# A decoder layer on one core: scores issued ahead of the PV in front of them, late row work placed anew, and a tail on ScalarE

## The chip, the cores and the metric

The kernel runs on one core of one Trainium2 chip. The metric is the device time of one execution in microseconds (us). The core has five engines with a queue each: PE (TensorE, matrix products), DVE (VectorE), ACT (ScalarE), POOL (GpSimd) and SP (SyncE, which only issues DMAs). They run in parallel and wait for each other through semaphores.

## The reference

The input `x` is 8 batches x 256 rows x 512 features, float32; `ctx` has the same shape.

```python
x = layernorm(x + attention(x))        # 16 heads of 32, softmax over 256 keys, then Wo
r_t = decay * r_{t-1} + ctx_t**2       # per feature, a recurrence along the 256 rows
x = layernorm(x + x * r)
g, u = x @ gate_w.T, x @ up_w.T        # 2048 wide; the three weights are cubic splines
x = layernorm(x + (silu(g) * u) @ down_w.T)
```

## The kernel before, in words

Matrix products keep float32 accuracy by splitting each operand into a high and a low part; each product is three matmuls (lines 303 to 305). The order of the work on every engine is written out by hand, as one function for each piece and engine (`pe_...`, `act_...`, `dve_...`, `pool_...`); each engine takes its queue strictly in that order.

**Attention.** The loop runs over batches `b` = 0 to 7. A batch has four quarters `m` = 0 to 3 of four heads each. A quarter is a chain over the engines:

- S on PE (`pe_s`, line 478): the scores of four heads into four banks of PSUM; minus the maximum of each row on DVE (`dve_max`, line 821); the exponential with row sums on ACT (`act_exp`, line 665);
- T on PE (`pe_t`, line 490): 16 transposes of the probabilities; copies back by ACT (line 677, head group 0) and DVE (line 835, three of them, `dve_heads`);
- R on PE (`pe_r`, line 498): the inverse row sums, spread by DVE (`dve_inverse`, lines 827 and 830), transposed; PV on PE (`pe_pv`, line 512); the product with the inverse on DVE (`dve_y`, line 785), then its high part on ACT (`act_yh`, line 673).

Between these steps PE has other work to cover the chain: the Q, K and V products of the next batch, Wo of the last one, and single matmuls for the spline weights (`pe_extra`). In batch 7 there is no next batch (`proj` is false). The recurrence is one scan per 128 features on DVE (`dve_scan`, line 896), four for a batch. POOL does the rest of the layer norms of a batch: `pool_norm1`, `pool_times`, `pool_scaled` and `pool_norm2`. DVE supplies them: `dve_stats(b, 0)` and `(b, 1)` give the mean and variance that norm1 and norm2 wait for, `dve_size(b)` the scale. SP stores the rows that norm2 finishes to DRAM (`x`, line 1070).

**FFN.** Four blocks `n` of 512 rows, two batches each; a block has eight steps `g` of 256 of the 2048 features, written (n, g). A step makes gate and up (`pe_gate_up`), silu on ACT, the product with up on DVE (`dve_hm`, line 1398), its high part on ACT and low part on DVE (line 1402), and the down product (`pe_down`), which runs one step behind. In block 0 a step also holds up to four *jobs*: each builds a piece of weights from spline coefficients. A job of the down weights needs a table, `makers_out`, that POOL fetches (`pool_makers_out(g)`, lines 1150 and 1151). `AHEAD_JOBS` of them are done before the first step. SP loads the rows of a block again (`x_in`, line 1228), to be transposed by PE (line 1165). POOL loads the block's residual rows, 1 MB, by `pool_res(n)` (line 1490); DVE adds the result of down to them (`dve_add`, line 1408), in the first step of the block that follows. Two of the four adds stand ahead of the second `dve_hm` of that step.

**Tail.** For the last block: add, statistics and `dve_out` (line 1426) per 128 rows on DVE, root and inverse on POOL (lines 1638 and 1640), and four stores that POOL issues at the end (line 1482).

## Time and profile before

| | us |
|---|---|
| median of 3 runs | 684.94 (684.87 to 685.00) |
| the profiled execution | 685.51 |
| its span | 683.7 |
| PE busy | 656.8 (96%) |
| DVE busy | 449.5 (66%) |
| ACT busy | 347.7 (51%) |
| POOL busy | 294.3 (43%) |
| mean granted clock of PE | 0.995 |

The span is the time from the first to the last instruction in the trace; 1.8 us of the execution lie outside it. Busy time is summed per engine. The end of a matmul in the trace is modelled: two that follow one another overlap in it (a 512-column matmul lasts 0.39 us in a row, and the next starts 0.23 us after it). So distances are read from start to start. The projections run to 63.6 us together with batch 0, batches 1 to 6 to 326.5, batch 7 to 367.3, first FFN pieces to 385.5, block 0 of the FFN to 458.5, and blocks 1 to 3 to 673.4, PE's last matmul.

### The profile page before, as it was taken

What the parts mean: (1) busy time and instruction counts of PE and PEld (TensorE: products, weight loads), DVE (VectorE), ACT (ScalarE), POOL (GpSimd) and SP (SyncE); (2) the same over time, 40 slices, a digit from 0 to 9 for tenths busy, and PEclk for the clock granted to TensorE, in tenths of its full rate; (3) what the DMA queues carried; (4) which work ended last, traced back from release to release, by engine and by line L of the source; (5) the groups of instructions that cost most, each with busy time, mean ns of one, the idle gap of its engine ahead of it and who ended that gap; (6) DMA issues with size and microseconds to landing.
All of it is one profiled execution on the core that took longest, in us unless ns stands there. A gap on an engine that the chain in (4) does not pass through costs nothing.

```text
span 683.7 us, 12025 instructions
## 1 busy us (share of the span) xinstructions
PE 656.8 (96%) x4312; PEld 533.8 (78%) x4312; DVE 449.5 (66%) x826; ACT 347.7 (51%) x1002; POOL 294.3 (43%) x351
## 2 busy tenths in 40 slices
PE   9999999999999999999988799999999999999993
PEld 9597887878888788788865577888888888888883
DVE  3567687698686877878778688666544555354434
ACT  5566546637466565656667556552334233333230
POOL 1764486886638767594674836100100001000103
PEclk9999999999999999999999999999999999999997
DMA  9621020030220311121112672741193317340301
GB/s 329 221 80 62 1 87 7 2 125 1 94 62 2 133 52 32 63 72 41 40 65 47 159 173 72 210 105 40 35 239 78 81 32 198 72 101 0 124 1 61
DMA packets 22010, 58.06 MB, mean 85 GB/s; under 512 B 4032, under 2 KB 7232, under 8 KB 21056
## 3 DMA queue, kind: packets, MB, share of 16 engines
q1 hardware_dynamic: 16720, 44.45, 22.5%
q0 software_dynamic: 4944, 12.32, 5.9%
q8 instruction: 35, 0.57, 0.3%
q10 hardware_dynamic: 288, 0.52, 0.2%
q14 instruction: 23, 0.19, 0.1%
HBM read 32.11 MB, written 8.39 MB: 59 GB/s over the span
## 4 chain that ended last, share of the span: by engine, by line
PE 78%; DVE 12%; ACT 6%; issue 2%; POOL 1%; DVEq 0%; POOLq 0%; ACTq 0%
PE bank L303 19%; PE bank L305 18%; PE bank L304 18%; PE bank L490 6%; ACT probs L665 5%; PE bank L478 4%; DVE recurrence_T L896 4%; PE bank L512 4%; DVE minus_max L821 3%; PE bank L1191 2%; PE bank L1096 2%; DVE probsT L835 2%; PE bank L529 1%; PE bank L316 1%; PE bank L498 1%
## 5 line engine op out<-in xcount | busy, mean ns | idle before, releaser
L665 ACT ACTIVATE probs<-bank,minus_max 128x256 f32<-128x256 f32 x256 | 117.3, 486 | 23.8 <-DVE minus_max L821 23.8
L303 PE MATMUL bank<-down,hidden_hi_lo 128*128 128x512 f32 x256 | 100.7, 393 | 1.5 <-DVE hidden_hi_lo L1402 1.5
L305 PE MATMUL bank<-down,hidden_hi_lo 128*128 128x512 f32 x256 | 100.5, 392 | 0.0
L304 PE MATMUL bank<-down,hidden_hi_lo 128*128 128x512 f32 x256 | 100.0, 391 | 0.0
L821 DVE TENSOR_REDUCE minus_max<-bank 128x2 f32<-128x512 f32 x128 | 79.3, 681 | 16.3 <-PE bank L478 16.3
L1398 DVE TENSOR_TENSOR hidden<-bank,silu 128x512 f32<-128x512 f32 x64 | 44.1, 689 | 60.9 <-PE bank L305 58.9
L1356 ACT ACTIVATE silu<-bank 128x512 f32<-128x512 f32 x64 | 38.3, 598 | 82.2 <-PE bank L305 81.3
L1402 DVE TENSOR_TENSOR hidden_hi_lo<-hidden,hidden_hi_lo 128x512 fp32r<-128x512 f32 x64 | 45.5, 711 | 40.9 <-ACT hidden_hi_lo L1369 40.8
L490 PE MATMUL bank<-ident,probs 128*128 128x128 f32 x512 | 65.5, 275 | 6.2 <-ACT probs L665 5.9
L1476 POOL TENSOR_TENSOR ffn_var_eps<-ffn_mean_var,constants 128x4 f32<-128x4 f32 x3 | 0.6, 196 | 156.5 <-DVE ffn_mean_var L1418 156.5
L490 PEld LDWEIGHTS bank<-ident,probs 128*128 128x128 f32 x512 | 56.6, 141 | 14.2 <-ACT probs L665 12.0
L1369 ACT CAST hidden_hi_lo<-hidden 128x512 fp32r<-128x512 f32 x64 | 39.8, 622 | 52.3 <-DVE hidden L1398 52.3
L835 DVE COPY probsT<-bank 128x512 f32<-128x512 f32 x96 | 60.1, 680 | 4.8 <-PE bank L490 4.7
L303 PEld LDWEIGHTS bank<-down,hidden_hi_lo 128*128 128x128 f32 x256 | 48.1, 188 | 11.5 <-DVE hidden_hi_lo L1402 1.9
L305 PEld LDWEIGHTS bank<-down,hidden_hi_lo 128*128 128x128 f32 x256 | 48.0, 188 | 10.3
L665 ACT ACTIVATION_READ_ACCUMULATOR probs<-bank,minus_max 128x1 f32 x256 | 55.9, 219 | 0.0
L304 PEld LDWEIGHTS bank<-down,hidden_hi_lo 128*128 128x128 f32 x256 | 48.1, 188 | 9.7
L303 PE MATMUL bank<-xT_hi_lo,wq_hi 128*128 128x256 f32 x128 | 38.7, 303 | 1.1 <-DVE spline_coef_T_down L773 0.4
L303 PE MATMUL bank<-xT_hi_lo,wk_hi 128*128 128x256 f32 x128 | 38.9, 304 | 0.0
L512 PE MATMUL bank<-probsT,V 128*32 128x256 f32 x512 | 36.8, 385 | 0.4 <-ACT inverse_by_query L680 0.4
L478 PE MATMUL bank<-k_heads,q_heads 32*128 32x256 f32 x512 | 36.7, 400 | 0.0
L305 PE MATMUL bank<-xT_hi_lo,wq_lo 128*128 128x256 f32 x128 | 36.1, 282 | 0.0
(170 smaller groups left out, 1610.8 us busy)
## 6 DMA issues: line engine op xcount, KB each, us to landing
features_by_group<-features_by_cell SPq DMA_DIRECT2D x128, 128.0 KB, 2.4
ctx_squared_T<-in_ctxT SPq DMA_DIRECT2D x8, 512.0 KB, 3.3
xres<-in_x SPq DMA_DIRECT2D x8, 512.0 KB, 4.6
x_in<-x SPq DMA_DIRECT2D x16, 256.0 KB, 3.1
x_residual<-x POOLq DMA_DIRECT2D x4, 1024.0 KB, 8.1
out_x<-x_residual POOLq DMA_DIRECT2D x16, 256.0 KB, 2.8
xin_T<-in_xT SPq DMA_DIRECT2D x7, 512.0 KB, 3.9
x<-x_rows SPq DMA_DIRECT2D x7, 512.0 KB, 4.1
```

What stands on the lines that cost most here:

```text
L303: nc.tensor.matmul(out, wh, xh, start=first, stop=False)
L304: nc.tensor.matmul(out, wh, xl, start=False, stop=False)
L305: return nc.tensor.matmul(out, wl, xh, start=False, stop=last)
L478: last = nc.tensor.matmul(S[g][:, t * T:(t + 1) * T], qk[0][at, m, t * P:(t + 1) * P], qk[1][at, m, :], start=True, stop=True)
L490: last = nc.tensor.transpose(S[g][:, kt * T + t * P:kt * T + (t + 1) * P], probs[:, g, t, kt * P:(kt + 1) * P], ident[:])
L512: last = nc.tensor.matmul(MI[g * DH:(g + 1) * DH, 0:T], V[:, kt, h * DH:(h + 1) * DH], probsT[:, g, kt, :], start=kt == 0, stop=kt == TT - 1)
L665: inc(nc.scalar.activation(probs[:, g, t, :], S[g][:, t * T:(t + 1) * T], ACT.Exp, bias=nmax[:, g, t:t + 1], accum_out=rsum[:, t, g:g + 1] ...
L821: inc(nc.vector.tensor_reduce(nmax[:, g, :], S[g][:].rearrange("p (t k) -> p t k", t=TT), AX.X, ALU.max, negate=True), "max")
L835: inc(nc.vector.tensor_copy(probsT[:, g, :, :], S[g][:].rearrange("p (k t) -> p k t", k=2)), "ptv")
L1369: inc(nc.scalar.copy(hid[:, g % 2, 0, j, :], hm[:]), "hh")
L1398: inc(nc.vector.tensor_tensor(hm[:], U[:], sg[:], ALU.mult), "hm")
L1402: inc(nc.vector.tensor_tensor(hid[:, g % 2, 1, j, :], hm[:], hid[:, g % 2, 0, j, :].bitcast(F32), ALU.subtract), "hl")
```

## The change

1. *S before PV.* On PE, S of quarter m+1 is issued ahead of PV of quarter m. DVE takes the maxima of quarter m+1 ahead of `dve_y` of m, and ACT makes the high part of y inside the exponentials of the next quarter, ahead of the fourth head.
2. *Scan.* The four scans of batches 0 to 6 go from behind `dve_heads(2)` to ahead of `dve_inverse(2)`; those of batch 7 go behind job 16, after the batch.
3. *Row work of batches 6 and 7.* The table of places:

| | before | now |
|---|---|---|
| `dve_stats(6, 1)` | ahead of the FFN | end of step (0, 1) |
| `dve_size(6)` | batch 7 | behind job 17 |
| `dve_stats(7, 0)` | end of (0, 0) | end of (0, 2) |
| `dve_size(7)` | end of (0, 2) | end of (0, 5) |
| `dve_stats(7, 1)` | end of (0, 3) | end of (0, 7) |
| `pe_rs(7)`, `act_rs1(7)` | ahead of features 2 and 3 | behind job 18 |

4. *Makers.* POOL's transfers `pool_makers_out(2)` to `(7)` stand at other places between the norms, and `pool_res(0)`, which was last, still is, but now directly behind `pool_norm2(7)`.
5. *Wo.* The last low part of Wo (`wo_lo`) is made inside the maxima of quarter 1 of batch 0.
6. *Jobs.* 20 instead of 19 are done ahead; step (0, 0) has its job elsewhere.
7. *Tail.* The last normalization is an ACT instruction (identity with scale and bias) per 128 rows, for which POOL makes minus mean times inverse as a third small operation; SP issues the four stores, each when its rows are there.

```diff
+
+        pe_s(pe, b, 1)
         if b == 0:
             pe_fold_o(pe, 3)
         pe_pv(pe, b, 0)
-
-        pe_s(pe, b, 1)
         pe_q(pe, b, 2)
         pe_k(pe, b, 2)
         pe_q(pe, b, 3)
...
             act.wait_ge(s["max"], 16 * b + 4 * m + g + 1)
             for t in range(TT):
                 inc(nc.scalar.activation(probs[:, g, t, :], S[g][:, t * T:(t + 1) * T], ACT.Exp,
@@ -708,7 +710,6 @@
         if post:
             act_rs1(act, b - 1)
         act_extra(act, b, 0)
-        act_yh(act, b, 0)
 
...
         if b == 0:
-            for m in range(MT):
+            for m in range(MT - 1):
                 dve_weight_lo(dve, "o", m)
+        dve_max(dve, b, 1)
         dve_y(dve, b, 0)
-        dve_max(dve, b, 1)
         dve_extra(dve, b, 0)
         if post:
             dve_stats(dve, b - 1, 0)
         dve_inverse(dve, b, 1)
         dve_heads(dve, b, 1)
 
+        dve_max(dve, b, 2)
         dve_y(dve, b, 1)
-        dve_max(dve, b, 2)
         dve_extra(dve, b, 1)
-        if not proj:
-            dve_scan(dve, b, range(2))
+        if proj:
+            dve_scan(dve, b)
         dve_inverse(dve, b, 2)
         dve_heads(dve, b, 2)
-        if proj:
-            dve_scan(dve, b, range(KT))
-        else:
+
+        dve_max(dve, b, 3)
+        dve_y(dve, b, 2)
+        if not proj:
             dve_x2l(dve, 0, 0, B_)
             dve_x2l(dve, 0, 1, C_)
-
-        dve_y(dve, b, 2)
-        dve_max(dve, b, 3)
         dve_extra(dve, b, 2)
-        if post:
+        if post and proj:
             dve_size(dve, b - 1)
-        if not proj:
-            dve_scan(dve, b, range(2, KT))
         dve_inverse(dve, b, 3)
         dve_heads(dve, b, 3)
...
+    def dve_scan(dve, b):
+        dve.wait_ge(s["csq"], 2 * b + 2)
+
+        wait(dve, "rs", 2 * b)
+        for k in range(KT):
             inc(nc.vector.tensor_tensor_scan(rsT[:, k, :], dec[:, k:k + 1].to_broadcast([P, T]),
...
-        if post:
+        if post and b < B - 1:
             pool_scaled(pool, b - 1)
...
-    AHEAD_JOBS = 2 * NG + 3
+    AHEAD_JOBS = 2 * NG + 4
...
             if n == 0:
-                pe.wait_ge(s["wld"], 2 * JT * g + 1)
+                wait(pe, "wld", 2 * JT * g)
+                pe.wait_ge(s["wl"], AHEAD_JOBS)
...
-        i = AHEAD_JOBS + (2 * JT * g - 2 + k if g else k)
-        return i if n == 0 and i < NJOB and (g or k < 2) else None
+        i = AHEAD_JOBS + (2 * JT * g - 3 + k if g else k)
+        return i if n == 0 and i < NJOB and (g or k < 1) else None
...
@@ -1337,13 +1334,13 @@
         pe_gate_up(pe, n, g, 0)
         pe_turn(pe, n, g, 0)
         pe_down(pe, prev, 0)
-        pe_fill(pe, n, g, 0)
+        if prev:
+            pe_fill(pe, n, g, 0)
         pe_down(pe, prev, 1)
-        if prev:
-            pe_fill(pe, n, g, 1)
+        pe_fill(pe, n, g, 1)
         pe_turn(pe, n, g, 1)
         pe_gate_up(pe, n, g, 1)
-        pe_fill(pe, n, g, 2 if prev else 1)
+        pe_fill(pe, n, g, 2 if prev else 0)
...
-        act_fill_hi(act, n, g, 0)
         if before(n, g):
+            act_fill(act, n, g, 0)
+            act_fill_hi(act, n, g, 0)
             act_fill(act, n, g, 1)
             act_turn(act, n, g, 1)
             act_fill_hi(act, n, g, 1)
             act_silu(act, n, g, 1)
+            act_fill(act, n, g, 2)
+            act_hh(act, n, g, 1)
         else:
             act_silu(act, n, g, 1)
-            act_fill(act, n, g, 1)
-            act_fill_hi(act, n, g, 1)
-        act_fill(act, n, g, 2)
-        act_hh(act, n, g, 1)
+            act_hh(act, n, g, 1)
+            act_fill(act, n, g, 0)
+            act_fill_hi(act, n, g, 0)
...
     def dve_out(dve, n, t):
-        if n < NB - 1:
-            dve.wait_ge(s["rstd"], n + 1)
-        else:
-            wait(dve, "rstd", NB + t)
+        dve.wait_ge(s["rstd"], n + 1)
...
-        dve_fill(dve, n, g, 0)
-        if ends:
-            dve_add(dve, n - 1, 1)
-        dve_fill_lo(dve, n, g, 0)
         if before(n, g):
+            dve_fill(dve, n, g, 0)
+            if ends:
+                dve_add(dve, n - 1, 1)
+            dve_fill_lo(dve, n, g, 0)
             dve_fill(dve, n, g, 1)
             dve_turn(dve, n, g, 1)
             dve_fill_lo(dve, n, g, 1)
             dve_hm(dve, n, g, 1)
+            dve_fill(dve, n, g, 2)
+            dve_hl(dve, n, g, 1)
         else:
             dve_hm(dve, n, g, 1)
-            dve_fill(dve, n, g, 1)
-            dve_fill_lo(dve, n, g, 1)
-        dve_fill(dve, n, g, 2)
-        dve_hl(dve, n, g, 1)
+            dve_hl(dve, n, g, 1)
+            dve_fill(dve, n, g, 0)
+            dve_fill_lo(dve, n, g, 0)
...
         if n == 0:
-            if g == 0:
+            if g == 1:
+                dve_stats(dve, B - 2, 1)
+            elif g == 2:
                 dve_stats(dve, B - 1, 0)
-            elif g == 2:
+            elif g == 5:
                 dve_size(dve, B - 1)
-            elif g == 3:
+            elif g == 7:
                 dve_stats(dve, B - 1, 1)
...
+            pe_rs(pe, B - 1, 0)
+            pe_rs(pe, B - 1, 1)
+            pe.wait_ge(s["ws"], 2 * NG + 3)
+            pe_job(pe, 2 * NG + 3, X)
...
-            act_fh(act, 0, 0, B_)
-            act_fh(act, 0, 1, C_)
-            act_rs1(act, B - 1)
-            act_fh(act, 0, 2, A_)
-            act_fh(act, 0, 3, B_)
+            for q, out in enumerate((B_, C_, A_, B_)):
+                act_fh(act, 0, q, out)
             act_job_hi(act, 2 * NG - 1)
             for i in range(2 * NG, AHEAD_JOBS):
                 act_job(act, i, X)
                 act_job_hi(act, i)
+                if i == AHEAD_JOBS - 2:
+                    act_rs1(act, B - 1)
...
+            for t in range(BT):
+                act.wait_ge(s["nm"], t + 1)
+                inc(nc.scalar.activation(res[:, t, :], res[:, t, :], ACT.Identity, bias=fnm[:, t:t + 1], scale=frstd[:, t:t + 1]), "yout")
...
-            dve_fl(dve, 0, 3, B_)
+            for q, out in enumerate((B_, C_, A_, B_)):
+                dve_fl(dve, 0, q, out)
             dve_job(dve, 2 * NG, X)
+            dve_scan(dve, B - 1)
             dve_r1(dve, B - 1, 0)
             dve_job(dve, 2 * NG + 1, X)
+            dve_size(dve, B - 2)
             dve_r1(dve, B - 1, 1)
             dve_job(dve, 2 * NG + 2, X)
+            dve_job(dve, 2 * NG + 3, X)
...
                     dve_step(dve, n, g)
@@ -1592,9 +1594,6 @@
                 dve_out_stats(dve, NB - 1, t)
                 dve.wait_ge(s["bn"], BT * (NB - 1) + t + 1)
                 inc(nc.vector.bn_aggr(fmv[:, t, :], fst6[:, t, :]), "mv")
-                if t:
-                    dve_out(dve, NB - 1, t - 1)
-            dve_out(dve, NB - 1, BT - 1)
...
             for i in range(2 * NG - 1, AHEAD_JOBS):
                 pool_job_lo(pool, i)
+            pool_scaled(pool, B - 2)
+            pool_makers_out(pool, 2)
             pool_norm2(pool, B - 2)
-            pool_makers_out(pool, 2)
+            pool_makers_out(pool, 3)
             pool_norm1(pool, B - 1)
+            pool_makers_out(pool, 4)
             pool_times(pool, B - 1)
-            pool_makers_out(pool, 3)
-            pool_makers_out(pool, 4)
+            pool_makers_out(pool, 5)
+            pool_makers_out(pool, 6)
             pool_scaled(pool, B - 1)
-            pool_makers_out(pool, 5)
+            pool_makers_out(pool, 7)
             pool_norm2(pool, B - 1)
-            pool_makers_out(pool, 6)
-            pool_makers_out(pool, 7)
             pool_res(pool, 0)
...
@@ -1638,9 +1638,9 @@
                 inc(nc.gpsimd.tensor_tensor(fve[:, t:t + 1], fmv[:, t, 1:2], half[:, 0, 0:1], ALU.add), "ve")
                 pool.wait_ge(s["ve"], NB + t)
                 inc(nc.gpsimd.tensor_tensor(frstd[:, t:t + 1], fve[:, t:t + 1], half[:, 2, 0:1], ALU.pow), "rstd")
-            for t in range(BT):
-                pool_out(pool, NB - 1, t)
-            pool.wait_ge(s["out"], 16 * BT * NB)
+                pool.wait_ge(s["rstd"], NB + t)
+                inc(nc.gpsimd.tensor_scalar(fnm[:, t:t + 1], fmv[:, t, 0:1], frstd[:, t:t + 1], -1.0, ALU.mult, ALU.mult), "nm")
+            pool.wait_ge(s["out"], 16 * BT * (NB - 1))
...
+            for t in range(BT):
+                sp.wait_ge(s["yout"], BT * (NB - 1) + t + 1)
+                inc(sp.dma_start(out_v[:, BT * (NB - 1) + t, :], res[:, t, :]), "last", 16)
+            sp.wait_ge(s["last"], 16 * BT)
```

**PE, batch 1, around the scores of quarter 1.** L478 are the scores, L512 is PV, L529 and L402 are pieces of other work. Before:

```order
L498 MATMUL bank<-ident,row_sum_inverse_wide 128x128 x2
L529 MATMUL bank<-ident,recurrence_T 128x128 x4
L402 MATMUL bank<-ident,spline_coef_rows 128x128 x4
L512 MATMUL bank<-probsT,V 32x256 x8
L478 MATMUL bank<-k_heads,q_heads 128x256 x8
L303 MATMUL bank<-xT_hi_lo,wq_hi 128x256
```

Now:

```order
L498 MATMUL bank<-ident,row_sum_inverse_wide 128x128 x2
L529 MATMUL bank<-ident,recurrence_T 128x128 x4
L402 MATMUL bank<-ident,spline_coef_rows 128x128 x4
L478 MATMUL bank<-k_heads,q_heads 128x256 x8
L512 MATMUL bank<-probsT,V 32x256 x8
L303 MATMUL bank<-xT_hi_lo,wq_hi 128x256
```

The two groups have changed places; nothing else moved there.

**DVE, batch 1, quarters 2 and 3.** Before (L896 in the profile is the scan):

```order
L827 RECIPROCAL row_sum_inverse<-row_sum 128x8
L830 COPY row_sum_inverse_wide<-row_sum_inverse 128x256
L835 COPY probsT<-bank 128x512 x3
L896 SCALAR_TENSOR_TENSOR recurrence_T<-decay,ctx_squared_T 128x256 x4
L785 TENSOR_TENSOR heads_out<-bank,inverse_by_query 128x256
L821 TENSOR_REDUCE minus_max<-bank 128x2 x4
```

Now (the scan is L892, the inverse L828 and L831, the copies L836):

```order
L822 TENSOR_REDUCE minus_max<-bank 128x2 x4
L784 TENSOR_TENSOR heads_out<-bank,inverse_by_query 128x256
L772 CAST spline_coef_T_up<-bank 128x512
L892 SCALAR_TENSOR_TENSOR recurrence_T<-decay,ctx_squared_T 128x256 x4
L828 RECIPROCAL row_sum_inverse<-row_sum 128x8
L831 COPY row_sum_inverse_wide<-row_sum_inverse 128x256
L836 COPY probsT<-bank 128x512 x3
L822 TENSOR_REDUCE minus_max<-bank 128x2 x4
L784 TENSOR_TENSOR heads_out<-bank,inverse_by_query 128x256
```

The scans stand ahead of the inverse and the three copies of quarter 2 now, behind the maxima of that quarter.

**POOL, from the first norm of batch 7 to the residual load.** Before (of the small operations of `pool_norm2(7)` the last is shown):

```order
L957 TENSOR_SCALAR residual_odd<-residual_odd,mean_var,rstd 128x512 x2
L965 TENSOR_TENSOR residual_odd<-residual_odd,recurrence_plus_one 128x512 x2
L1150 DMA makers_out<-in_makers 128x256
...
L995 TENSOR_TENSOR rstd_kept<-rstd,keep 128x2
L1002 TENSOR_SCALAR recurrence_plus_one<-residual_odd,mean_var,rstd_kept 128x512 x2
L1150 DMA makers_out<-in_makers 128x256
L1151 DMA masks_out<-in_masks 128x256
L1150 DMA makers_out<-in_makers 128x256
L1151 DMA masks_out<-in_masks 128x256
L1490 DMA x_residual<-x 128x2048
```

Now:

```order
L998 TENSOR_SCALAR x_rows<-residual_even,mean_var,rstd_kept 128x512 x2
L1146 DMA makers_out<-in_makers 128x256
L1147 DMA masks_out<-in_masks 128x256
L947 TENSOR_TENSOR var_eps<-mean_var,constants 128x2
L949 TENSOR_TENSOR rstd<-var_eps,constants 128x2
L953 TENSOR_SCALAR residual_odd<-residual_odd,mean_var,rstd 128x512 x2
...
L991 TENSOR_TENSOR rstd_kept<-rstd,keep 128x2
L998 TENSOR_SCALAR recurrence_plus_one<-residual_odd,mean_var,rstd_kept 128x512 x2
L1488 DMA x_residual<-x 128x2048
```

The second norm of batch 6 (`x_rows`) is now followed directly by table 3, which stood behind `pool_times(7)`. Tables 6 and 7 went ahead of the second norm of batch 7, which now stands directly ahead of the residual load.

## Rows read from the trace of the kernel before

The columns of a timeline are the start in us, the duration in us, engine, line, operation, output<-input, and in brackets the idle time ahead of it with what ended it. The columns of a windows view are the stretch, its length, then busy time (and instructions) of PE, PE's weight load, DVE, ACT and POOL, the granted clock of PE, the DMA share and GB/s.

**Rows 1.** windows of PE's span; length, busy of each engine, clock, DMA share, GB/s
```profile
63.60:326.50 262.90, 258.77 (x2189) 212.05 (x2188) 201.62 (x378) 157.16 (x554) 182.67 (x197) 1.00 0.15 50
326.50:385.50 59.00, 51.19 (x375) 37.90 (x373) 46.34 (x94) 38.92 (x121) 36.24 (x48) 1.00 0.25 66
385.50:458.50 73.00, 71.93 (x340) 58.17 (x341) 55.61 (x111) 43.88 (x97) 27.11 (x34) 1.00 0.53 142
458.50:673.40 214.90, 214.88 (x953) 175.48 (x951) 107.09 (x180) 71.89 (x120) 13.51 (x25) 1.00 0.32 82
```

**Rows 2.** waits of PE, 20 to 326.5 us: total, times, longest
```profile
PE bank L490 <- ACT probs L665: 2.8, 11, 0.3
...
PE bank L303 <- DVE spline_coef_T_down L773: 0.4, 2, 0.2
```

**Rows 3.** timeline of PE in batch 1: start, duration, operation
```profile
91.62 1.91 PE L490 MATMUL bank<-ident,probs 128*128 128x128 f32 x16
...
94.08 0.39 PE L498 MATMUL bank<-ident,row_sum_inverse_wide 128*128 128x128 f32 x2
...
95.78 1.07 PE L512 MATMUL bank<-probsT,V 128*32 128x256 f32 x16
...
102.25 0.66 PE L490 MATMUL bank<-ident,probs 128*128 128x128 f32 x4
103.16 0.66 PE L490 MATMUL bank<-ident,probs 128*128 128x128 f32 x4 [0.25 <-ACT probs L665]
```

**Rows 4.** timeline of DVE in batch 1
```profile
94.50 5.73 DVE L896 TENSOR_TENSOR_SCAN recurrence_T<-decay,ctx_squared_T 128x256 f32<-128x256 f32 x4
```

**Rows 5.** the scan's line L896: min/median/max ns over the program
```profile
L896 DVE TENSOR_TENSOR_SCAN recurrence_T<-decay,ctx_squared_T x32: 657/1026/2505, 51.5 to 363.0; 128x256 f32<-128x256 f32 x32
```

**Rows 6.** timeline of DVE in FFN step (0, 1)
```profile
396.52 0.68 DVE L1211 TENSOR_TENSOR features_by_cell<-bank,features_by_cell 128x512 fp32r<-128x512 f32 x1
```

**Rows 7.** timeline of POOL, second norm of batch 7
```profile
419.62 0.19 POOL L983 TENSOR_TENSOR var_eps<-mean_var,eps 128x2 f32<-128x2 f32 x1 [2.69 <-DVE mean_var L801]
...
426.96 0.61 POOL L1150 DMA_DIRECT2D makers_out<-in_makers  x1
...
437.77 0.53 POOL L1490 DMA_DIRECT2D x_residual<-x  x1
```

**Rows 8.** DMA issues, 386 to 391 us: KB each, us to landing
```profile
x_in<-x SPq DMA_DIRECT2D x2, 256.0 KB, 4.3
```

**Rows 9.** timeline of PE at the end of step (0, 2)
```profile
404.81 0.60 PE L1165 MATMUL bank<-ident,x_in 128*128 128x128 f32 x4
```

**Rows 10.** timeline of DVE at the end of block 0
```profile
457.97 0.69 DVE L1211 TENSOR_TENSOR features_by_cell<-bank,features_by_cell 128x512 fp32r<-128x512 f32 x1
...
462.10 1.44 DVE L1408 TENSOR_TENSOR x_residual<-bank,x_residual 128x512 f32<-128x512 f32 x2
464.24 0.69 DVE L1398 TENSOR_TENSOR hidden<-bank,silu 128x512 f32<-128x512 f32 x1 [0.69 <-PE bank L305]
```

**Rows 11.** timeline of PE, group 1 of block 1
```profile
467.47 0.39 PE L303 MATMUL bank<-features_by_group,spline_coef_T_up 128*128 128x512 f32 x1
```

**Rows 12.** DMA issues, 436 to 447 us
```profile
x_residual<-x POOLq DMA_DIRECT2D x1, 1024.0 KB, 8.5
```

**Rows 13.** DMA issues, 640 to 652 us
```profile
x_residual<-x POOLq DMA_DIRECT2D x1, 1024.0 KB, 5.0
```

**Rows 14.** windows at the start and after the last matmul
```profile
1.50:7.70 6.20, 6.20 (x29) 6.20 (x30) 1.66 (x3) 3.44 (x5) 0.07 (x3) 1.00 0.91 299
...
673.40:676.70 3.30, 0.00 (x0) 0.00 (x0) 3.16 (x8) 0.00 (x0) 1.32 (x4) 1.00 0.00 0
676.70:683.70 7.00, 0.00 (x0) 0.00 (x0) 0.80 (x2) 0.00 (x0) 3.14 (x6) 0.50 0.40 150
```

**Rows 15.** timelines of the end: DVE
```profile
676.44 0.52 DVE L1426 TENSOR_SCALAR x_residual<-x_residual,ffn_mean_var,ffn_rstd 128x512 f32<-128x512 f32 x1
```

**Rows 16.** timelines of the end: POOL
```profile
677.58 2.34 POOL L1482 DMA_DIRECT2D out_x<-x_residual  x4
```

26 lines of the change are left out of this document (8 added, 18 removed).

## The prediction

> **What bounds the kernel now.** First the windows of the trace, for PE's busy time in each stage. Blocks 1 to 3 of the FFN have no hole: 214.88 us busy of 214.9. Block 0 loses 1.1 of 73.0, batches 1 to 6 lose 4.1 of 262.9, and only batch 7 with the first FFN pieces loses much, 7.8 of 59.0 [rows 1]. So PE bounds nearly everything, no matmul is added or removed, and the change can win little ahead of the tail. It can lose without limit wherever it puts a wait in front of PE. Second, the waits of PE, for what ends them: in the batches the transposes, held up by ACT's exponentials, and the products behind a spline coefficient that DVE casts [rows 2]. Third, the timelines where the change moves something, above all the last DVE and POOL work of block 0. Fourth, the end after the last matmul, 10.3 us in which PE does nothing.
>
> All sums are against the profiled execution, 685.51 us (span 683.7 and 1.8 around it). It lies 0.57 above the median 684.94; I take that off at the end.
>
> **S before PV, batches 0 to 6.** A held group of four transposes starts 0.91 us after the one before it; 16 transposes without a wait last 1.91 us, 0.109 from start to start and 0.44 a group [rows 3]. So each of the 11 waits before 326.5 costs 0.47: 5.2 us. PV lasts 1.07 us, 1.0 to the start of the next [rows 3]; with S ahead of it the exponentials start that much earlier, and in batch 1 three waits of 0.47, 1.4 in all, were there to gain. The six spline waits of 0.2 idle cost 0.35 each, start to start: 2.1 more, since the cast no longer stands behind a late y. Gain at most 7.3. (The windows show 4.1 idle there, because the modelled ends of matmuls cover part of each hole; starts are the better measure.)
>
> Against it, the scan. In batch 1 four scans take 5.73 us behind the copies of quarter 2, and PE meanwhile does other products [rows 4]. Moved ahead of the inverse, they start at about 89.4 (behind maxima and the cast, y no longer in the way) and end at 95.1 at that pace; then 0.7 for the reciprocal and the spread row. R is issued at 94.08 [rows 3], so PE waits 1.8, and S of quarter 3, which needs the copies, 0.2 more. At the shortest scan, 0.66, they end at 92.0 and nothing waits; the median is 1.03 [rows 5]. Per batch 0 to 2.0. I take 1.1 in batches 1, 2 and 3, 0.3 in batch 0 and nothing in 4 to 6, where the same reading leaves slack: 3.6 in all; 0 to 9 as bounds. Net -3.7; with 0.3 for the last low part of Wo, which comes earlier into reach of batch 0, I take **-4.0** (-7 to +2).
>
> The scan has two inputs in the SBUF memory. The trace shows it between 0.66 and 2.51 us for one size [rows 5], the long ones beside POOL operations. The Trainium skill, "SBUF — State Buffer", "Who interferes with whom", says that a DVE instruction with two SBUF inputs contends with a GpSimd instruction that reads SBUF, one blocking the other. The trace agrees. By that rule the price of the moved scan depends on what POOL does at the new place, and the upper bound of each batch stands; by a fixed cost per scan it would be nothing.
>
> **Batch 7 to the end of step (0, 1).** The scans leave the batch, which frees waits of some 1.5, but they now stand with `dve_size(6)` (1.2 and two small ones) between jobs 16 and 19 on DVE, and job 19 itself is new ahead of the first down product: 2.7 + 1.6 of DVE work in front of a PE that has only Wo and two jobs left. I set the one against the other: +0.1 (-3 to +3; all that is idle there is 7.8 [rows 1]). In steps (0, 0) and (0, 1): job 20 placed late +0.2, POOL's norm of batch 7 no longer beside DVE -0.6, `dve_stats(6, 1)` at the end of (0, 1) +1.0. Sum **+0.7**.
>
> **Table 3 and x_in, step (0, 2).** `dve_stats(6, 1)` now runs behind the last feature copy of (0, 1), which starts at 396.52 [rows 6]: two statistics and aggregates, 1.65 us, so its result is there at about 398.2. `pool_norm2(6)` waits for it and takes what it takes for batch 7: 419.62 to 426.96, 7.3 [rows 7]. Behind it, from 405.5, stand table 3 on POOL and on SP the store of batch 6 with two `x_in` loads behind it, which land after 4.3 [rows 8]. PE wants `x_in` at 404.81 [rows 9] and table 3 just ahead of it; they come at about 409 to 410. With the 0.7 of above already late, PE waits **+3.5** (2 to 4.5).
>
> **Steps (0, 2) to (0, 7).** Statistics of batch 7 at the end of (0, 2): +0.3. Table 4 is issued behind norm1(7), which waits for those statistics; it lands some 1.5 after job 32 wants it: +1.5 (0 to 2.5). `dve_size(7)` and table 7: +0.7 together (0 to 1). Sum **+2.5**.
>
> **The residual of block 0.** This is the largest term. Before, `pool_norm2(7)` was done at 426.96 and the load was issued at 437.77 [rows 7], 24 us before DVE wanted it, at 462.10 [rows 10]. Now `dve_stats(7, 1)` comes at the end of step (0, 7), after the copy that ends at 458.66 [rows 10], and adds 1.65: 460.3. Norm2 takes 7.3, to 467.7. Only then does POOL issue the load. It lands 8.5 after its issue [rows 12] with the store of batch 7 and two `x_in` beside it, and the same two are released with it now: 476.2. DVE is strictly in order: two adds (1.44), then `dve_hm` of step (1, 0), which releases the bank that "up" of group 1 fills. It ended at 464.93 and will end at 478.3. PE wants the bank at 467.47 [rows 11]: 10.9 lost. The down product then waits for the low part, 0.7 more than "up" of 0.7 hides. Together 11.6, against a nominal time that already moved with the terms above; nothing else shortens it, as DVE follows PE's banks by under 1 us there (its wait of 0.69 in [rows 10]). Bounds: the last of the four residual loads, alone in the queues, landed in 5.0 [rows 13], which makes 8.1; 1 us more than 8.5 makes 12.6. I take **+11.7**.
>
> **The clock.** PE's granted clock was 1.00 (2.4 GHz) through the 3.3 us after the last matmul and 0.50 (1.2 GHz) in the 7.0 behind them [rows 14]. An idle PE of some 11 us would meet this. At the start, 29 matmuls of the size of a transpose took 6.2 us [rows 14], 0.21 each against 0.109 in [rows 3]. If the same comes back, half of 6.2 us is lost, 3.1. But the one group "up" falls into the wait, and the shorter waits of batch 7, 7.8 us in all, cost no clock [rows 1]. **+2.0** (0 to 3.1). The Trainium skill, "TensorE: Matmul & The Clock Gate", "Part 1: The HAM clock gate", says that the default state is throttled and activity releases it. By that rule the loss comes for certain after the long wait, and the sum would be 1.1 higher.
>
> **Tail.** Three of DVE's outputs stand between adds and statistics, 0.52 us each; the third starts at 676.44 [rows 15], right behind the last aggregate. The two ahead of that, 0.43 each from start to start, delay it: -0.9. POOL then takes 0.4 and 0.5, and a third small one of 0.3 to 0.5 comes in: +0.4. ACT's normalization replaces DVE's (0.55); ACT's casts of 128x512 took 0.6: 0. POOL issued four stores in a row, 2.34 us, from 677.58 [rows 16], and the last landed 3.1 after its own issue. SP issues each when its rows are there, so three of the issues (1.6) lie beside other work. The end comes after the landing either way. -2.1, and -0.3 as POOL's own wait is off the path: **-2.4** (-1.5 to -3). An activation table might have to be loaded; the trace has none on ACT between silu and identity-like copies in the FFN, so I take nothing for it.
>
> **Sum.** -4.0 + 0.7 + 3.5 + 2.5 + 11.7 + 2.0 - 2.4 = +14.0; 685.5 + 14.0 = 699.5 profiled, less 0.57: **698.9 us**, slower by 2.0%.
>
> **Rivals.**
> A, *faster*: the residual load is no wait. For that DVE would have to finish step (0, 7) 11 us or more ahead of PE's need, or POOL to reach the norm earlier. From 11.6 us of slack on it costs nothing; below, the difference. Then the table and `x_in` of step (0, 2) would be covered as well, and the time is 684.9 - 4.0 + 0.7 + 0.5 - 2.4 = 679.7. Against it: DVE follows PE by under 1 us in [rows 10]. Chance 0.06.
> B, *the load is short and the clock holds*: 8.1 in place of 11.7, and no clock term: 684.9 + 14.0 - 3.6 - 2.0 = 693.3. For it: the load that is alone lands in 5.0 [rows 13]. Against it: the same companions as at 437.77. Chance 0.24.
> C, *the scans eat the batches*: the moved scan costs 2.0 in each of batches 1 to 5, 10.0 in place of 3.6: 684.9 + 14.0 + 6.4 = 705.3. For it: POOL is as busy there in batches 4 and 5. Chance 0.12.
> D, *the clock falls at both long waits*, also at the 3.5 of step (0, 2), which is as long as the 3.3 that passed at full clock: 3.1 twice in place of 2.0: 703.1. Chance 0.08.
> The forecast, with its neighbours of 2 us either side: 0.49. The rest, 0.01, near no change.
>
> The change may also not do all that it says in the batches: if S still waits for what PV waited for, the gain of 5.2 is gone; that gives 704.1 and counts with C.
>
> **How the numbers follow.** Low end: B with a further 3 from the bounds of the batches, 690. High end: C with 0.7 more, 706. The forecast's own range is 695.5 to 702.5. A measurement tells 0.2% (1.4 us) from no change here. Faster only by A and by an edge of the batches' gain: 0.07; within 0.2%: 0.02; slower: 0.91.
>
> **What would show it.** Right: a DVE `x_residual` add in the first step of block 1 that waits some 10 us for the DMA, with the residual load issued at about 467 plus the shift, directly behind norm2; PE idle for that long ahead of "up" of group 1; a granted clock under 1 behind it; another PE wait of about 3 us at `x_in` or job 28; the waits of transposes on ACT gone from the batches, and new ones at line 498 on the inverse row in batches 1 to 3; a tail shorter than 8.3 us from the last matmul. Wrong: the load lands before the add is due. Then the sum falls by two thirds and more, and everything hangs on batches and tail, which favour the change.

## The result, and the profile after

The changed kernel takes 701.19 us (median of 4 runs, 697.83 to 702.46), against 684.97 for the kernel before in the same comparison: ratio 1.0229, 95% interval 1.0194 to 1.0265. It is slower by 16.2 us; the whole interval lies above 1, and whether it is 2% or a little less stays open. The profiled execution took 701.36 with a span of 699.6.

How far the changed kernel is ahead of or behind the one before, read from the start of the same DVE instruction in both traces (maxima in the attention, `dve_hm` in the FFN):

| place | shift, us |
|---|---|
| batch 2, quarter 0 | -2.9 |
| batch 4, quarter 0 | -5.9 |
| batch 6, quarter 2 | -9.9 |
| batch 7, quarter 0 | -7.0 |
| first down product | -6.8 |
| FFN step (0, 2), second half | -7.2 |
| (0, 3), first half | -0.9 |
| (0, 3), second half | +6.9 |
| (0, 7), second half | +8.9 |
| (1, 0), second half | +21.6 |
| (1, 1), second half | +21.0 |
| (3, 7), second half | +19.4 |
| end of the span | +15.8 |

From batch 6 on, 0.5 us of each entry belong to the profiled execution of the kernel before: its PV of batch 5 (282.7 to 283.6) ran 0.5 longer than in e4, e6, e9 and e10, whose work there is the same. Without it the end is at +16.3, as the medians have it.

Attention gains 7 to 10 us, three places in the FFN lose 27, and blocks 1 to 3 and the tail give 5 back. The waits of PE in the changed kernel name the three places (columns as in [rows 2]):

```profile
PE bank L303 <- DVE hidden L1396: 10.2, 1, 10.2
PE bank L1161 <- DMA x_in<-x: 5.9, 1, 5.9
PE bank L1092 <- DMA makers_out<-in_makers: 5.8, 2, 4.6
...
PE bank L498 <- DVE row_sum_inverse_wide L831: 1.9, 1, 1.9
PE bank L478 <- DVE probsT L836: 1.7, 3, 1.2
...
PE bank L490 <- ACT probs L667: 1.1, 3, 0.6
```

The last row answers to the first of [rows 2]: of the transposes' waits on the exponentials almost nothing is left. L1161 is the transpose of `x_in`, L1092 a job with table 3.

**The residual load.** POOL, the changed kernel:

```profile
469.16 0.19 POOL L979 TENSOR_TENSOR var_eps<-mean_var,eps 128x2 f32<-128x2 f32 x1 [15.90 <-DVE mean_var L800]
...
472.17 4.15 POOL L998 TENSOR_SCALAR recurrence_plus_one<-residual_odd,mean_var,rstd_kept 128x512 f32<-128x512 f32 x2
476.27 0.61 POOL L1488 DMA_DIRECT2D x_residual<-x  x1
```

DVE and PE behind it:

```profile
470.37 0.69 DVE L1400 TENSOR_TENSOR hidden_hi_lo<-hidden,hidden_hi_lo 128x512 fp32r<-128x512 f32 x1 [0.69 <-ACT hidden_hi_lo L1366]
484.58 1.29 DVE L1406 TENSOR_TENSOR x_residual<-bank,x_residual 128x512 f32<-128x512 f32 x2 [13.53 <-DMA x_residual<-x]
485.79 0.68 DVE L1396 TENSOR_TENSOR hidden<-bank,silu 128x512 f32<-128x512 f32 x1
```

```profile
486.52 0.80 PE L303 MATMUL bank<-features_by_group,spline_coef_T_up 128*128 128x512 f32 x1 [10.18 <-DVE hidden L1396]
```

The load is issued 5.2 us after the add could have run (471.06, behind the row at 470.37) and lands 8.3 later. DVE stands 13.5 us in front of the add, with the `hm` that PE waits for behind it in its queue. These rows answer to [rows 7, 10, 11].

**Step (0, 2).** POOL and SP's queue in the changed kernel:

```profile
390.55 0.19 POOL L979 TENSOR_TENSOR var_eps<-mean_var,eps 128x2 f32<-128x2 f32 x1 [9.92 <-DVE mean_var L800]
...
397.89 0.62 POOL L1146 DMA_DIRECT2D makers_out<-in_makers  x1
```

```profile
397.97 0.33 SPq L1066 DMA_DIRECT2D x<-x_rows  x1
398.39 1.24 SPq L1224 DMA_DIRECT2D x_in<-x  x2
399.67 10.55 SPq L1216 DMA_DIRECT2D features_by_group<-features_by_cell  x16
410.26 1.08 SPq L1224 DMA_DIRECT2D x_in<-x  x2
```

PE:

```profile
401.99 0.77 PE L1092 MATMUL bank<-spline_coef_T_down,makers_out 128*128 128x256 f32 x2 [4.56 <-DMA makers_out<-in_makers]
...
417.31 1.12 PE L1161 MATMUL bank<-ident,x_in 128*128 128x128 f32 x4 [5.91 <-DMA x_in<-x]
```

POOL waits 9.9 us for the statistics of batch 6 and then needs 7.3 for norm2. Table 3 is issued behind it, at 397.89, and PE waits 4.6 for it. The store and the first `x_in` pair are late as well, and so are the 16 feature transfers behind them; only behind these comes the second pair, which PE wants at 411.4. It lands 7.0 after its issue. In the kernel before the order on SP is the same, but the 16 transfers start at 391.74, the second pair is issued at 405.55, and PE uses it without a wait at 411.98.

**The clock.** Windows of the changed kernel:

```profile
350.50:353.10 2.60, 0.07 (x4) 0.01 (x1) 2.60 (x6) 2.60 (x13) 0.00 (x0) 1.00 0.00 0
353.10:356.50 3.40, 3.38 (x18) 3.22 (x19) 1.39 (x5) 3.37 (x10) 1.50 (x2) 0.61 0.00 0
...
397.30:402.00 4.70, 0.14 (x2) 0.04 (x1) 1.03 (x2) 0.41 (x2) 1.77 (x3) 0.96 0.72 205
402.00:411.30 9.30, 8.96 (x38) 7.22 (x38) 5.30 (x12) 3.75 (x8) 3.64 (x4) 0.84 1.04 215
411.30:417.30 6.00, 0.10 (x1) 0.00 (x0) 0.87 (x2) 0.37 (x1) 5.01 (x5) 0.83 0.98 205
417.30:418.60 1.30, 1.29 (x5) 1.25 (x6) 0.00 (x0) 0.13 (x1) 0.00 (x0) 0.50 0.05 14
418.60:423.00 4.40, 4.40 (x14) 3.52 (x13) 2.76 (x5) 2.65 (x6) 0.40 (x1) 0.60 0.00 0
...
476.00:486.50 10.50, 0.35 (x2) 0.00 (x0) 1.89 (x3) 0.00 (x0) 0.89 (x2) 0.70 0.90 250
486.50:492.00 5.50, 5.47 (x16) 4.17 (x17) 3.18 (x5) 1.74 (x3) 0.00 (x0) 0.65 1.06 217
```

The granted clock fell from 2.4 to 1.2 GHz at each of the three long waits, also at the one of 4.6 us, and came back some us into the work that followed: 0.84 over 9.3 us, 0.50 and 0.60 over 5.7, 0.65 over 5.5. Work in these stretches ran longer by the missing share: 1.5, 2.4 and 1.9 us, 5.8 in all. The Trainium skill, "TensorE: Matmul & The Clock Gate", "Part 1: The HAM clock gate", says that the throttled clock is the default and that activity releases it; the trace agrees at these three places.

The first two rows are batch 7, where the clock fell as well (0.61 over 3.4 us), behind a wait of 2.6 that had another of 1.2 ahead of it. The traces with this wait of 2.6 (the changed kernel, e1, e2 and e8) all show it, but batch 7 can lose clock without the change too. In the profiled execution of the kernel before there is no fall; in e6, which has the same instructions and the same waits there (0.8 and 1.05, against 0.8 and 1.04), the clock is half for 3.4 us. Before, then e6, the windows and the PV in them:

```profile
364.90:368.30 3.40, 3.03 (x22) 1.41 (x22) 2.93 (x7) 1.88 (x6) 3.01 (x5) 1.00 0.00 0
365.33 1.95 PE L512 MATMUL bank<-probsT,V 128*32 128x256 f32 x16 [0.22 <-ACT inverse_by_query L680]
```

```profile
364.90:368.30 3.40, 3.40 (x18) 1.73 (x15) 2.20 (x4) 1.02 (x4) 2.32 (x5) 0.50 0.00 0
364.63 2.81 PE L512 MATMUL bank<-probsT,V 128*32 128x256 f32 x16 [0.22 <-ACT inverse_by_query L680]
```

So between executions of the same work the clock falls behind a wait of 1 us or does not. It costs 0.9 us there, and the executions of the kernel before that were taken beside the experiments stand in two groups that fit: 684.7 to 685.4 with a mean clock of 0.994 to 0.996, and 685.7 to 686.0 with 0.991 to 0.994 (one of 1075 us at 0.556, a slow one, is left out).

**The tail.** SP and ACT at the end of the changed kernel, and the landing of the four stores:

```profile
692.60 4.86 SPq L1694 DMA_DIRECT2D out_x<-x_residual  x4
```

```profile
696.30 0.81 ACT L1563 ACTIVATE x_residual<-x_residual,ffn_minus_mean,ffn_rstd 128x512 f32<-128x512 f32 x1 [0.71 <-POOL ffn_minus_mean L1642]
```

```profile
out_x<-x_residual SPq DMA_DIRECT2D x4, 256.0 KB, 2.0
```

SP issues the four over 4.9 us, each when its rows are there, and they land in 2.0 us (median; 2.8 in the kernel before, from POOL).

### The profile page after: what moved, and what is told of

It is laid out like the page before. It is cut to its first block, busy times and chain, and to the rows that moved or that the text cites. A ratio compares the mean times of both kernels' runs of the same rounds, so it can differ in the third digit from the quotient of the medians.

```text
span 699.6 us, 12030 instructions
## 1 busy us (share of the span) xinstructions
PE 654.8 (94%) x4312; PEld 538.0 (77%) x4312; DVE 441.9 (63%) x821; ACT 349.6 (50%) x1006; POOL 293.0 (42%) x352
## 4 chain that ended last, share of the span: by engine, by line
PE 81%; DVE 7%; POOL 3%; DMA 3%; ACT 2%; issue 2%; SPq 2%; DVEq 0%; POOLq 0%; ACTq 0%
PE bank L303 19%; PE bank L304 18%; PE bank L305 18%; PE bank L490 8%; PE bank L478 5%; PE bank L512 4%; PE bank L1187 2%; SPq L1216 1%; PE bank L1092 1%; DMA x_residual<-x 1%; PE bank L498 1%; DMA x_in<-x 1%; PE bank L1161 1%; PE bank L402 1%; PE bank L529 1%
## 5 line engine op out<-in xcount | busy, mean ns | idle before, releaser
L667 ACT ACTIVATE probs<-bank,minus_max 128x256 f32<-128x256 f32 x256 | 118.7, 487 | 41.0 <-DVE minus_max L822 41.0
L836 DVE COPY probsT<-bank 128x512 f32<-128x512 f32 x96 | 60.3, 681 | 10.3 <-PE bank L490 10.3
L490 PE MATMUL bank<-ident,probs 128*128 128x128 f32 x512 | 63.1, 277 | 1.1 <-ACT probs L667 1.1
L490 PEld LDWEIGHTS bank<-ident,probs 128*128 128x128 f32 x512 | 58.6, 143 | 4.2 <-ACT probs L667 1.8
L303 PEld LDWEIGHTS bank<-down,hidden_hi_lo 128*128 128x128 f32 x256 | 48.9, 191 | 10.7 <-DVE hidden_hi_lo L1400 1.3
L305 PEld LDWEIGHTS bank<-down,hidden_hi_lo 128*128 128x128 f32 x256 | 48.6, 190 | 10.5
L304 PEld LDWEIGHTS bank<-down,hidden_hi_lo 128*128 128x128 f32 x256 | 48.8, 191 | 9.2
L917 POOL TENSOR_TENSOR yT_lo<-heads_out,yT_hi 128x256 fp32r<-128x256 f32 x24 | 20.0, 835 | 60.5 <-ACT yT_hi L675 60.5
L478 PE MATMUL bank<-k_heads,q_heads 32*128 32x256 f32 x512 | 36.7, 399 | 2.3 <-DVE probsT L836 1.7
L682 ACT COPY inverse_by_query<-bank 128x256 f32<-128x256 f32 x32 | 11.9, 373 | 52.0 <-PE bank L498 52.0
```

Of the source, the lines that this page charges most:

```text
L303: nc.tensor.matmul(out, wh, xh, start=first, stop=False)
L304: nc.tensor.matmul(out, wh, xl, start=False, stop=False)
L305: return nc.tensor.matmul(out, wl, xh, start=False, stop=last)
L478: last = nc.tensor.matmul(S[g][:, t * T:(t + 1) * T], qk[0][at, m, t * P:(t + 1) * P], qk[1][at, m, :], start=True, stop=True)
L490: last = nc.tensor.transpose(S[g][:, kt * T + t * P:kt * T + (t + 1) * P], probs[:, g, t, kt * P:(kt + 1) * P], ident[:])
L667: inc(nc.scalar.activation(probs[:, g, t, :], S[g][:, t * T:(t + 1) * T], ACT.Exp, bias=nmax[:, g, t:t + 1], accum_out=rsum[:, t, g:g + 1] ...
```

## The experiments

All ratios are to the kernel before, run beside the same group: e1 to e4 (median 685.03), e5 to e8 (685.25), e9 to e11 (684.97). Differences of times from two groups carry these 0.3 us. The diffs are excerpts; "..." marks what is left out.

**e1: row work of batches 6 and 7, and POOL's order of norms, tables and residual load, as before; all else as changed** (parts 3 and 4 without `pe_rs(7)` and `act_rs1(7)`).

```diff
-        if post and proj:
+        if post:
             dve_size(dve, b - 1)
...
-            if g == 1:
-                dve_stats(dve, B - 2, 1)
+            if g == 0:
+                dve_stats(dve, B - 1, 0)
             elif g == 2:
-                dve_stats(dve, B - 1, 0)
-            elif g == 5:
                 dve_size(dve, B - 1)
-            elif g == 7:
+            elif g == 3:
                 dve_stats(dve, B - 1, 1)
...
+            dve_stats(dve, B - 2, 1)
...
-            dve_size(dve, B - 2)
...
-            pool_scaled(pool, B - 2)
+            pool_norm2(pool, B - 2)
             pool_makers_out(pool, 2)
-            pool_norm2(pool, B - 2)
+            pool_norm1(pool, B - 1)
+            pool_times(pool, B - 1)
             pool_makers_out(pool, 3)
-            pool_norm1(pool, B - 1)
...
```

> The changed kernel with the row work of batches 6 and 7 (statistics, sizes, scaled) and POOL's order of norms, tables and residual load as before; all else as changed. Theory W (three late DMAs behind the late row work cost about 21 us of PE and the clock some 5 more): the waits at table 3, at both pairs of x_in and at the residual add go, 24 of 701.2, so 677 (675 to 680), and PE's granted clock is 1.00 through block 0. Theory J (the twentieth job ahead and the new order of step (0, 0) cost the time): the time stays above 690.

676.90 us, ratio 0.9878 (0.9863 to 0.9893). All three long waits are gone, as theory W has it, and theory J's 690 falls. The new places of the row work and of what POOL does behind it cost 24.3 us; e1 puts both back, so it does not share this out between statistics and tables. W's clock of 1.00 through block 0 was missed by one stretch: it was half from 385.7 to 389.1, behind a wait of 1.9 for a job's weights on DVE.

**e2: only the residual load put ahead.**

```diff
+            pool_res(pool, 0)
             pool_norm2(pool, B - 1)
-            pool_res(pool, 0)
```

> The changed kernel with only the residual load of block 0 ahead of the second norm of batch 7. Theory W: the wait of 10.2 us ahead of up of group 1 goes and the half-speed stretch behind it (1.9), so 689 (687.5 to 690.5), with the waits of step (0, 2) unchanged. Rival L (the load lands late whatever its place, because the queues are full there): 698 to 701.

689.58 us, ratio 1.0055 (1.0037 to 1.0074): 11.6 less than the changed kernel, from two lines exchanged, and inside W's range. L falls. The waits of step (0, 2) remain: 4.5 and 5.0 in its trace.

**e3: the swap alone on the kernel before.**

```diff
+        pe_s(pe, b, 1)
         if b == 0:
             pe_fold_o(pe, 3)
         pe_pv(pe, b, 0)
-
-        pe_s(pe, b, 1)
...
+        dve_max(dve, b, 1)
         dve_y(dve, b, 0)
-        dve_max(dve, b, 1)
```

> The kernel before with part 1 of the change alone (S ahead of PV, maxima ahead of y, high part of y ahead of the fourth head, Wo's last low part): scan, row work, jobs and tail as before. Theory S (the swap itself gains the batches): 5 to 7 of the 9.9 us, so 678 to 680. Rival R (the scan's move gains them, since the scan of quarter 2 holds the maxima of quarter 3): the waits of the last transposes of batches 1 to 3 stay, and the time is 682 to 684.

685.98 us, ratio 1.0012 (1.0002 to 1.0021): nothing gained. Both numbers missed; R's mechanism was seen, though. The waits of the transposes stay (6.7 us, 18 of them; 5.9 and 19 before), since DVE still takes the scan ahead of the maxima of quarter 3:

```profile
95.15 5.56 DVE L897 TENSOR_TENSOR_SCAN recurrence_T<-decay,ctx_squared_T 128x256 f32<-128x256 f32 x4
100.63 2.45 DVE L822 TENSOR_REDUCE minus_max<-bank 128x2 f32<-128x512 f32 x4
```

**e4: the tail alone on the kernel before**, the diff of part 7.

> The kernel before with the tail alone (last normalization on ACT, stores by SP). Theory T (the profile's 3.6 us are the tail's own): 681.4 (681 to 681.8). Rival (some of it came with the shifted PE): 682.5, my forecast's 2.4.

679.25 us, ratio 0.9916 (0.9901 to 0.9931): 5.8 less, where 3.6 was expected. From the last matmul on the trace gains the 3.6. The other 2.2 lie in FFN steps that the edit does not touch: their 512-column matmuls follow each other faster (e6, e9, e10).

**e5: the moved scan alone on the kernel before.**

```diff
-        if not proj:
+        if proj:
+            dve_scan(dve, b, range(KT))
+        else:
             dve_scan(dve, b, range(2))
         dve_inverse(dve, b, 2)
         dve_heads(dve, b, 2)
-        if proj:
-            dve_scan(dve, b, range(KT))
-        else:
+        if not proj:
             dve_x2l(dve, 0, 0, B_)
             dve_x2l(dve, 0, 1, C_)
```

> The kernel before with the scans of batches 0 to 6 ahead of the inverse and the copies of quarter 2, and nothing else. The swap alone gained nothing in the batches (+1.3 in its trace) and both together gained 9.9 up to batch 6. Theory P (each needs the other: with the scan where it was, the maxima of quarter 3 still come late, and with the scan moved but S behind PV the copies come late for PV): 684 to 687. Rival R (the scan alone gains it): 676 to 678.

689.32 us, ratio 1.0056 (1.0039 to 1.0073): slower by 4.1, above P's 684 to 687; R falls. PE waits at line 498 for the row that DVE spreads behind the scan, 8.8 us in five waits: 1.5, 2.3, 2.3 and 1.7 in batches 0 to 3, and 1.0 in batch 7 that was there before. Neither half gains; the two together gain 9.9 up to batch 6. Batch 1 shows how. DVE in e5:

```profile
91.14 5.55 DVE L896 TENSOR_TENSOR_SCAN recurrence_T<-decay,ctx_squared_T 128x256 f32<-128x256 f32 x4
```

DVE in the changed kernel, and POOL beside it:

```profile
87.75 3.29 DVE L892 TENSOR_TENSOR_SCAN recurrence_T<-decay,ctx_squared_T 128x256 f32<-128x256 f32 x4
```

```profile
88.36 1.18 POOL L917 TENSOR_TENSOR yT_lo<-heads_out,yT_hi 128x256 fp32r<-128x256 f32 x1 [1.59 <-ACT yT_hi L675]
89.50 1.00 POOL L905 CAST xT_hi_lo<-xin_T 128x512 fp32r<-128x512 f32 x1
```

With S and the maxima early, the scan starts 3.4 us earlier than in e5. There POOL is idle at first, and the four scans take 3.3 instead of 5.6. In batches 1 to 6 the four take 3.3 to 3.4 in the changed kernel; in e5 they take 5.6 in batches 1 to 3 and 2.4 in 4 to 6, where no wait at line 498 arises. The Trainium skill, "SBUF — State Buffer", "Who interferes with whom", says that a DVE instruction with two SBUF inputs contends with a GpSimd instruction that reads SBUF, and that the order of issue decides which one is held up. The trace fits: in the changed kernel POOL's operations beside the scans are the long ones (1.18 and 1.00, where the same two take 0.74 and 0.61 in e5, ahead of its scans), and the scans are not. Which of the two has to wait was not tested by itself.

**e6: 16 unused bytes.**

```diff
-    fve, frstd = sb("ffn_var_eps", [P, BT]), sb("ffn_rstd", [P, BT])
+    fve, frstd, unused = (sb(n, [P, BT]) for n in ("ffn_var_eps", "ffn_rstd", "unused"))
```

> The kernel before with one more small tile of 16 bytes for each partition, allocated where the changed tail has ffn_minus_mean, and used by nothing. In the tail-alone kernel the 512-column matmuls of the FFN followed each other in 0.227 us in place of 0.229, all through blocks 1 to 3. Theory A (the tile shifts the addresses of all the large tiles behind it, and PE reads them faster there): 0.227 here too and 2.2 to 2.7 us less, 682.5. Rival C (it comes from the code or the semaphores of the tail): 684.9.

682.75 us, ratio 0.9964 (0.9951 to 0.9977): 2.2 to 2.5 us from a tile that nothing uses. A holds.

**e7: swap, moved scan and tail on the kernel before** (e3, e5 and e4 together).

> The kernel before with swap, moved scan of batches 0 to 6 and tail; row work, makers, jobs ahead and the residual load as before. If the gains of the batches (9.9 until batch 6, of which 2 to 3 go again in batch 6) and of the tail-alone kernel (5.8) add: 671 (669 to 673). If batch 7 and the first steps need the new places of the change too: 674 to 677, like the kernel with only the row work put back.

673.79 us, ratio 0.9833 (0.9818 to 0.9847), between the two expectations, so neither was met. It is 3.1 below e1. What e1 has beyond it (the twentieth job and the order of step (0, 0), the scans and the row sums of batch 7 behind the jobs) therefore costs about 3, and J was right in that much; e1's wait of 1.9 for a job, with the clock behind it, is part of it.

**e8: the second pair of x_in earlier, in the changed kernel.**

```diff
                 for g in range(QUAD, NG):
                     sp_features(sp, 0, g, c)
+                if c == 0:
+                    for t in range(2, BT):
+                        sp_x2in(sp, 1, t)
             for n in range(1, NB):
                 for t in range(2, BT):
-                    sp_x2in(sp, n, t)
+                    if n > 1:
+                        sp_x2in(sp, n, t)
```

> The changed kernel with the second pair of x_in loads of block 1 issued behind the first 4 of the 16 feature transfers in place of behind all 16. Theory W2 (the wait of 5.9 us for the second pair comes from SP's order behind the late store, and the half-speed stretch behind it too): 701.2 less 6 to 8, so 694. Rival F (the DMA engines are full from 402 to 417, and the order among the transfers changes little): 699 to 701.

697.20 us, ratio 1.0169 (1.0154 to 1.0184): 4.0 less, in the direction of W2 and short of its 6 to 8. The wait on `x_in` (5.9) is gone. Part of what it gives comes back at once: waits of jobs on DVE are 5.0 in place of 2.0, one of them 2.8 long at 417.5, and the clock falls behind that one (half from 418.2 to 421.6).

**e9: the tail with all addresses held.**

```diff
-    fve, frstd, fnm = (sb(n, [P, BT]) for n in ("ffn_var_eps", "ffn_rstd", "ffn_minus_mean"))
+    fve, frstd = sb("ffn_var_eps", [P, BT]), sb("ffn_rstd", [P, BT])
...
     res = sb("x2_residual", [P, BT, D], F32, late)
+    fnm = sb("ffn_minus_mean", [P, BT], F32, late)
```

> The kernel before with the tail, but the small tile ffn_minus_mean allocated behind all other tiles, so that none of them moves. Theory A (16 bytes of shift gave 2.2 of the 5.8 us of the tail-alone kernel): the 512-column matmuls of gate and up follow each other in 0.229 to 0.231 us again, the stretch behind the last matmul stays 3.6 shorter, and the time is 681.4 (681.0 to 681.8). Rival C (code or semaphores of the tail speed up PE): 679.3 again.

681.50 us, ratio 0.9945 (0.9932 to 0.9958), as A has it. The tail is worth 3.5, and the other 2.2 of e4 are the shift of addresses; C falls.

**e10: 60 unused bytes.**

```diff
-    fve, frstd = sb("ffn_var_eps", [P, BT]), sb("ffn_rstd", [P, BT])
+    fve, frstd, unused = sb("ffn_var_eps", [P, BT]), sb("ffn_rstd", [P, BT]), sb("unused", [P, 15])
```

> The kernel before with an unused tile of 60 bytes for each partition in place of 16: the small tiles in front of the large ones then sum to a multiple of 64 bytes. Theory A1 (what counts is where the large tiles start within 32 or 64 bytes, and a multiple of 64 is no worse than the shift by 16): 682.7, gate and up at 0.227. Rival A2 (16 bytes hit one good place, 64 is as bad as before): 684.9 or more.

686.52 us, ratio 1.0019 (1.0010 to 1.0028): slower than with no pad, so A1 fell and A2's time came out. PE in e6, first and sixth matmul of a gate and up group:

```profile
661.77 0.39 PE L303 MATMUL bank<-features_by_group,spline_coef_T_gate 128*128 128x512 f32 x1
...
662.91 0.39 PE L305 MATMUL bank<-features_by_group,weights_lo_up 128*128 128x512 f32 x1
```

and in e10:

```profile
665.30 0.39 PE L303 MATMUL bank<-features_by_group,spline_coef_T_gate 128*128 128x512 f32 x1
...
666.46 0.40 PE L305 MATMUL bank<-features_by_group,weights_lo_up 128*128 128x512 f32 x1
```

Five steps take 1.14 in e6 and 1.16 in e10. Averaged over each of blocks 1 to 3, gate and up go at 0.227 us from start to start in e6, 0.230 to 0.231 in the kernel before and e9, 0.233 to 0.235 in e10; the matmuls of down at 0.227, 0.228 and 0.229.

**e11: e7 with the scan of batch 6 left behind the copies.**

```diff
-        if proj:
+        if proj and b < B - 2:
             dve_scan(dve, b, range(KT))
-        else:
+        elif not proj:
             dve_scan(dve, b, range(2))
         dve_inverse(dve, b, 2)
         dve_heads(dve, b, 2)
+        if proj and b == B - 2:
+            dve_scan(dve, b, range(KT))
         if not proj:
             dve_x2l(dve, 0, 0, B_)
```

> Swap, moved scan and tail on the kernel before (673.8), but the scan of batch 6 stays behind the copies of quarter 2. In the kernel with all seven moved, PE waited 1.9 at line 498 and 1.2 at the scores in batch 6 and lost 2.9 us there, while the swap with scans behind the copies lost 0.5. Theory M (POOL's operations beside it set what a scan and the copy behind it cost, and batch 6 is the one that pays): 671.5 (670.5 to 672.5). Rival (what batch 6 saves is lost to the maxima of quarter 3 and in batch 7): 673.5 to 675.

671.41 us, ratio 0.9796 (0.9782 to 0.9810), inside M's range and the best of all: 13.6 below the kernel before and 29.8 below the changed one. In e7 the spread row of batch 6, a copy, took ten times its usual 0.3 us beside a POOL operation, and PE waited 1.9 for it. In e11 it comes ahead of that operation and takes 0.3, and the wait is gone. That POOL's operation is what stretched the copy is read from the overlap. DVE and POOL in e7:

```profile
303.52 3.14 DVE L831 COPY row_sum_inverse_wide<-row_sum_inverse 128x256 f32<-128x256 f32 x1
```

```profile
303.98 2.52 POOL L966 TENSOR_TENSOR residual_odd<-residual_odd,recurrence_plus_one 128x512 f32<-128x512 f32 x2
```

DVE in e11:

```profile
301.82 0.30 DVE L831 COPY row_sum_inverse_wide<-row_sum_inverse 128x256 f32<-128x256 f32 x1
...
304.95 3.73 DVE L899 TENSOR_TENSOR_SCAN recurrence_T<-decay,ctx_squared_T 128x256 f32<-128x256 f32 x4
```

## Why the prediction was right, and where it was not

The direction, the main mechanism and the size were right: 698.9 forecast, 701.2 measured, 13.9 against 16.2. That the sizes agree to 2.3 us owes something to errors that cancel.

| term | forecast | measured |
|---|---|---|
| batches 0 to 6 | -4.0 | -7.0 |
| batch 7 to the end of (0, 1) | +0.7 | -0.2 |
| table 3 and x_in, step (0, 2) | +3.5 | +14.1 |
| rest of block 0 | +2.5 | +2.0 |
| residual load and the clock behind it | +13.7 | +12.1 |
| blocks 1 to 3 | 0 | -1.6 |
| tail | -2.4 | -3.6 |
| sum | +14.0 | +15.8 |

*The residual load* went as written: the statistics at the end of (0, 7), norm2 in 7.1, a landing after 8.3 (8.5 was taken), 10.2 of PE's time for 10.9, and 1.9 of clock for 2.0. e2 shows it by itself: 11.6 with the clock. The reasoning by queue order, from which DVE row stands ahead of which, was enough for the largest term.

*Table 3 and x_in* was the step that failed in size, four times too small. The sum held one wait. It named the store and "two `x_in` loads behind it" on SP, and stopped there: the 16 feature transfers behind these and the second `x_in` pair behind them were not counted. They brought a second wait of 5.9. The clock was charged only at the residual; it fell at both of these waits too (1.5 and 2.4). Rival D had the clock falling there, and that part of it came true. e8 shows that the second wait is due to SP's order, and how much of it comes back elsewhere.

*The batches* were right in sign and too small by 3 at their end, and the split behind the number was wrong in both halves. I gave the swap 7.3 and the scan -3.6, as if they added. e3 gives the swap nothing and e5 gives the scan -4.1; only together do they gain 9.9. PE's distances from start to start in batches 1 to 5, set against e9, whose work there is that of the kernel before, show which part failed. With both halves the transposes gave 5.3 (5.2 forecast) and the products behind the spline cast 3.1 (2.1 forecast), and all of PE 7.1. With the swap alone the products gave the same 3.1, but the transposes lost 1.5 and PV 2.3, and 0.2 was left. So the transposes' share of the 7.3 needed the scan out of the way of the maxima of quarter 3, which the sum did not ask for. The scan's price used 5.73 us, the duration at the old place; the new place beside an idle POOL made it 3.3. The waits at line 498 that I foresaw in batches 1 to 3 are there with the scan alone (e5) and not with both; in the changed kernel there is one, in batch 6 (1.9, and 1.2 at the scores), where I had taken nothing.

*The tail*: -2.4 forecast. The change's own is 3.5 (e9). The removed outputs and the overlapped issues were in the sum, which took a landing of 3.1 for SP's store; it was 2.0. ACT's instruction took 0.81 and not 0.55 to 0.6, 0.2 the other way.

*The clock*: the sum says that the shorter waits of batch 7 cost no clock. That holds for the one profiled execution; in e6 the same waits cost 0.9.

*Blocks 1 to 3*: no term at all. The 16 bytes of `ffn_minus_mean` moved every large tile and gave 2.2 in e6. No reading of the trace before could have shown it.

So the size came out partly by luck: table 3 and `x_in` were 10.6 too small, and batches, blocks 1 to 3, tail and the smaller terms together 8.8 too large.

## What to carry to other kernels

When a step moves later, follow its consumers through every in-order queue until the last instruction that was held, not only to the first one that is late. Two late loads on one queue are two waits, and each of the long waits of PE here also cost its clock. An edit that gains nothing alone may be half of one that does: the swap and the scan had to be tried together, and where DVE and POOL share work the duration of a moved step has to be read at the new place. Before crediting an edit with time in a stage that it does not touch, check whether it moved addresses.
